# The scan of a state in three pieces of one PSUM bank each, with three groups of turns

## What is computed

```python
def step(h, inp):
    dA_i, dB_i, u_i, C_i = inp
    h = dA_i * h + dB_i * u_i[:, :, None]
    y = jnp.einsum('bdn,bn->bd', h, C_i)
    return (h, y)
```

## Time and profile before

| | us |
|---|---|
| median of 2 runs | 3286.52 |
| lowest, highest | 3284.66, 3288.39 |
| the profiled execution | 3282.21 |
| its span, first to last instruction | 3280.3 |

### The profile page before, as it was taken

The page is one execution under the profiler, slowest core; times in us unless marked ns, Lnnn a source line. Parts: engine busy times, 40 slices in busy tenths (PEclk is TensorE's granted clock), DMA queues, the critical chain, the costliest instruction groups (busy, mean ns, idle before and its releaser), DMA issues. The chain is left out here.

```text
span 3280.3 us, 54538 instructions
## 1 busy us (share of the span) xinstructions
PE 2964.9 (90%) x19138; PEld 2406.4 (73%) x19138; DVE 2839.4 (87%) x4799; ACT 2710.2 (83%) x5234; POOL 2229.4 (68%) x911
## 2 busy tenths in 40 slices
PE   6999999999999999999999999999999997566664
PEld 4777787777777777777787878787887877455453
DVE  4889999999999999999999999999999998544442
ACT  5999999999999999999999999999999996211110
POOL 1777676666766666666767676767767676377776
PEclk8999999999999999999999999999999999688888
DMA  3112211222222222211222222212222111477774
GB/s 112 59 59 69 70 59 61 68 71 70 71 70 62 65 70 71 71 61 60 69 70 71 71 70 70 71 61 70 71 70 71 61 56 33 129 148 148 149 150 78
DMA packets 196175, 252.98 MB, mean 77 GB/s; under 512 B 45664, under 2 KB 174144, under 8 KB 195904
## 3 DMA queue, kind: packets, MB, share of 16 engines
q1 hardware_dynamic: 171328, 211.73, 20.6%
q0 software_dynamic: 24576, 37.77, 7.0%
HBM read 188.36 MB, written 61.08 MB: 76 GB/s over the span
## 5 line engine op out<-in xcount | busy, mean ns | idle before, releaser
L354 POOL TENSOR_TENSOR hid<-hid,c_all 128x1536 f32<-128x1536 f32 x512 | 1770.1, 3461 | 873.9 <-DVEq L617 872.4
L622 DVE TENSOR_TENSOR_SCAN hid<-decay,hid,psB 128x1024 f32<-128x1024 f32 x512 | 1201.5, 2347 | 76.9 <-PE psB L942 27.6
L397 ACT ACTIVATE decay<-dt,a_neg 128x383 f32<-128x383 f32 x2048 | 1085.3, 604 | 0.0
L942 PE MATMUL psB<-ident,dbu_t 128*128 128x128 f32 x5760 | 806.0, 276 | 82.4 <-DVE hid L622 67.6
L385 ACT ACTIVATE dbu_t<-dtu_t,b_t 128x512 f32<-128x512 f32 x1312 | 853.2, 714 | 17.7 <-PE psB L942 16.6
L942 PEld LDWEIGHTS psB<-ident,dbu_t 128*128 128x128 f32 x5760 | 657.6, 142 | 245.3 <-issue 113.5
L954 PE MATMUL psY<-ident,hid 128*128 128x128 f32 x6144 | 758.0, 273 | 1.0 <-POOL hid L354 1.0
L954 PEld LDWEIGHTS psY<-ident,hid 128*128 128x128 f32 x6144 | 690.7, 142 | 1.6 <-POOL hid L354 1.3
L622 DVE TENSOR_TENSOR_SCAN hid<-decay,psB 128x512 f32<-128x512 f32 x512 | 623.0, 1217 | 10.3 <-PE psB L942 6.3
L1024 PE MATMUL psM<-u,w_dt 128*128 128x384 f32 x1024 | 349.1, 489 | 4.8 <-ACT u L427 3.3
L1422 ACT ACTIVATE e_sg<-e_psU 128x256 f32<-128x256 f32 x64 | 24.5, 383 | 340.3 <-PE e_psU L1464 225.4
(11 more groups left out here) (156 smaller groups left out, 3570.1 us busy)
## 6 DMA issues: line engine op xcount, KB each, us to landing
c_all<-bc_rows_dram SPq DMA_DIRECT2D x128, 768.0 KB, 4.9
out_dram<-h SPq DMA_DIRECT2D x64, 384.0 KB, 3.0
h<-out_dram SPq DMA_DIRECT2D x32, 384.0 KB, 3.6
x_weights_dram<-normed SPq DMA_DIRECT2D x32, 384.0 KB, 2.6
xt<-in_x_t_dram SPq DMA_DIRECT2D x32, 375.0 KB
xs<-in_x_dram SPq DMA_DIRECT2D x32, 256.0 KB
e_wg<-in_gate_dram SPq DMA_DIRECT2D x64, 128.0 KB
e_wu<-in_up_dram SPq DMA_DIRECT2D x64, 128.0 KB
```

The source lines that it names most:

```text
L354: nc.gpsimd.tensor_tensor(hid[k % 4][:, :, :], hid[k % 4][:, :, :], c_all[:, k, :].unsqueeze(1).to_broadcast([P, CH, L]), ALU.mult).then_i ...
L397: last = nc.scalar.activation(decay[k % 4][:, c, 1:L], dt[q][:, c, 1:L], ACT.Exp, scale=a_neg[:, c, k:k + 1])
L622: nc.vector.tensor_tensor_scan(h[:, lo:hi], flat(decay[k % 4])[:, lo:hi], flat(psB)[:, lo:hi], h[:, lo - 1:lo] if j else 0.0, ALU.mult, AL ...
L942: last = nc.tensor.transpose(flat(psB)[:, i * P:(i + 1) * P], dbu_t[k % 2][:, t, c * P:(c + 1) * P], ident[:, :])
```

## The change

The three banks of `psB` become three pieces. PE's second group of turns (eight transposes) becomes two groups of four, called one behind the other in the same place, and DVE's second scan (1024 columns) becomes two of 512 columns, of which the last waits for the middle one and starts from its last column. Through `PB` = 3 all counts on `s_h` and `s_bt` grow from two to three a state.

```diff
--- before.py
+++ after.py
@@ -23,7 +23,7 @@
 NS = 16
 GN = 4
 NG = NS // GN
-PIECES = ((0, 1), (1, 3))
+PIECES = ((0, 1), (1, 2), (2, 3))
 PB = len(PIECES)
 CG = 4
 TAPS = 4
@@ -1096,6 +1096,7 @@
                             route(c)
                     if scans:
                         turn_dbu(b, q, k, 1)
+                        turn_dbu(b, q, k, 2)
                     if k == 0:
                         if front:
                             turn_normed1(n, 0)
```

## The result

The changed kernel takes 3426.95 us (median, 3421.98 to 3431.93), the kernel before 3286.52. The ratio is 1.0433, with a 95% interval of 1.0412 to 1.0453. A second set of runs on another occasion gave 3429.28 beside 3286.36 us, 1.0434 (1.0417 to 1.0451). The forecast was 3425 us.

The account below looks back on a forecast made before the run. DVE's own instructions were taken to pace the batch loop. The sum was 3280.3 + 162.3 - 24 = 3419 us of span, 3420.5 by execution time, then 4.3 more for the median: 3425 us, range 3400 to 3450.

Parts of the forecast that it names:

- The bound: Batch loop: DVE's own instructions set the pace, not PE; DVE time added lengthens it one to one, less its present waits.
- (a): Length of DVE's new carried 512-column scan pieces: taken as 1280 ns each, bounds 1217 and 1280.
- The second reading: DVE scan length: twice the ordinary slope per column, plus 63 ns for a start read from memory, thus 1280 ns.
- Rival 1: DVE's scan pieces: the carried start is free, a 512-column piece costs 1217 ns; 3360 us, chance 0.08.
- (b): DVE's scan: one more wait for its own piece, 181 ns a state (104 after the end beside 77 before).
- Rival 3: DVE's added wait for itself is free: each state grows by 136 ns; 3332 us, +1.4%, chance 0.04.
- (c): PE's finer turns shorten DVE's waits before the large piece: 24 us less, bounds 0 and about 45.
- (d): PE gets one wait and one increment more a state: costed at nothing, covered by 6.8 us idle a batch.
- (e): ACT and POOL count three pieces instead of two: both gain slack, costed at nothing.
- rival 2: PE's clock falls because PE idles more; at 0.90 a batch takes 92.2 us, 3499 us in all; chance 0.03.

## Why the prediction was right

**The bound.** The reading of the earlier trace rows against the earlier trace rows held: PE had the highest share and did not bind. Time added on DVE lengthened the loop, three groups of turns on PE alone did not (1.0002). The run with nothing carried adds what the prediction left open: of 4.3 us a batch taken from DVE only 1.1 came through, so the statement is true for added time and not for time taken away. There DVE waits more for PE, and POOL holds what stands behind the scans.

**(a) Length.** Right to the nanosecond: 1280. The second reading, an ordinary slope taken twice and about 60 ns for a start in memory, was measured directly by the constant start (1219 beside 1280). Rival 1 fell with it.

**(b) The wait.** The state came out at 3.91 us, 3908 ns, as summed. The share of the wait in it was put too low, 181 ns where the runs show 206, because the third piece without its wait is also 22 ns shorter itself; the prediction took the early start from the first pieces, which keep their length. The sum did not suffer, since it took the whole lengths of waiting pieces. Rival 3 fell: taking the wait away gave back 105.7 us over 512 states. That speaks against the sentence of the Trainium skill, "VectorE: DVE Perf Modes", section "The DRAIN you can't avoid", by which a semaphore in a chain costs nothing extra. It may hold for the chain that was measured there; here the wait for one's own result keeps the next operation from starting over the end of the last.

**(c) The relief.** Right in size, 162.3 - (3420.1 - 3280.3) = 22.5 us for 24, and wrong in its main cause, so that the size was in part luck. The prediction gave it mostly to the finer turning. The run with two groups of turns has the same time within its interval and the same 89.83 us a steady batch: most of the waits vanish because longer states on DVE give PE time. Per steady batch the relief is 5.07 - 4.81 = 0.26 us, 8 us over 32; the other 14 come from outside the steady middle, where DVE had idle time of its own.

**(d), (e) and the rest.** PE, ACT and POOL gained slack, as forecast; POOL's wait for the next scan grew from 872 to 1016 us. The clock stayed at 1.00 in the middle and the mean at 0.967, so rival 2 fell. Over all 31 intervals the batches are 89.2 us apart (104.9 to 2869.9), just under the 89.5 to 89.8 that was given; in the steady middle they are 89.83 apart, so the batches at the two ends absorb a part.

## What to carry to other kernels

Price the split of a recurrence by its three parts, read from the trace: here about 62 ns for the carried start, 206 for the wait for oneself and 48 for the instruction, so five sixths of it is the carry. Finer pieces pay only if the consumer waits for the producer longer than that; the idle time before the scans, 24 us beyond their own dependence over 512 states, said beforehand that at most 0.05 us a state was to be had for 0.32. Before work is moved into a gap on one engine, look at what another engine does in that stretch: an order that seems idle can be what keeps POOL beside operations that it does not hold up. The same care is due when those operations get shorter: at 3.40 us for two scans, POOL's 3.46 us already reached what stood behind them.

## What the runs showed of the hardware

- A scan piece that waits for the piece before it starts 104 ns after that one's recorded end. One that needn't wait starts about 80 ns before it (77 in the kernel before). The third piece without its wait took 22 ns less as well (1195 beside 1217); the first piece of a state, which stands behind the empty instruction, did not.
- A scan takes 151 + 2.083 ns a column with a constant start at 512, 768 and 1536 columns: 1217, 1739 and 3353 ns measured, 1218, 1751 and 3351 by the formula. At 768 the lengths lie between 1718 and 1756; the half that directly follows another piece is the shorter one.
- Two DVE instructions with two SBUF inputs that began beside POOL's product of 3.46 us, L734 and L655 in the rows shown, ended 0.81 and 0.02 us after it. In the mean the taps took 1208 ns for 606, the maximum 2574 for 234, L734 3388 for 934. The norms' scaling (one SBUF input) went from 404 to 795. Scans (PSUM and SBUF) and statistics (one SBUF input) kept their lengths.
